# Skip term of a selective-scan and feed-forward block: transposes of a scaled x in place of products with a diagonal, and jobs placed anew

## The chip, the cores and the metric

One core of one Trainium2 chip runs the whole program. The metric is the device time of one execution in microseconds, the median of several runs. A time is also given for the profiled execution, because the rows of the trace belong to that one.

## The reference, cut to what matters

```python
# x: (16, 1024, 256); W_xproj: (96, 256); W_dt: (256, 64); 16 states per channel
xz = einsum('btd,pd->btp', x, W_xproj)            # 64 rank columns, 16 B, 16 C
dt = softplus(einsum('btr,dr->btd', xz[..., :64], W_dt) + b_dt)
h_t = exp(dt_t * -exp(A_log)) * h_(t-1) + dt_t * B_t * x_t      # per channel, 16 states
y_t = sum_s h_t[s] * C_t[s]
x1  = layernorm(x + y + Dp * x)                   # the skip term: (1 + Dp) * x
out = layernorm(x1 + down(silu(gate(x1)) * up(x1)))             # hidden width 768
```

The change is about the term `(1 + Dp) * x`, with `x` in channel-major layout on the way to the token-major sum `y`.

## The kernel before, in words

**Tiles and chunks.** The 16 sequences of 1,024 tokens are cut into 32 chunks of 512 tokens. A chunk in channel-major layout is 128 partitions by 2 channel halves by 512 tokens. Two chunks make one sequence: the even one starts from state zero and its last column is saved (`carry`, L528 to L531), the odd one starts from that column. Even chunks carry sixteen small copies on ScalarE that odd ones lack, and in odd chunks the scans read `h_carry`.

**Work of a chunk, by engine.** A step is one state `s` of 16.
- ScalarE (ACT) makes the decay `exp(dt * -A)` (`decay`, L533 to L544), into the PSUM tile `p_da` for nine states and into the SBUF tile `da_k` for the seven of `K_STATES`. For those seven it also multiplies `u` by B in token-major layout (`ub_t`, L562), which TensorE transposes into `p_da` (L976).
- GpSimd (POOL) multiplies `u` by the broadcast B for the other nine states (`ub`, L434), multiplies `h` by the broadcast C for thirteen states (L445), and makes `u = dt * x` once (`u_of`, L424): 23 instructions a chunk.
- VectorE (DVE) runs two scans a state (L761), the product with C for three states (L770), and parts of the norms and of the feed-forward part.
- TensorE (PE) transposes each finished state and adds it into `p_y` (`sum_states`, L1009), adds the skip term there (`skip`, L1016 to L1021), and does the projections and the feed-forward products of the chunk before and of the one before that.

**What sets the order.** Each engine's program is written out by one loop over chunks, states and four or five zones of a step. `AT` (L34) names for each job the step and the zone in which every engine that has a part in it issues it. `DA_LEAD` (L57) says how many steps ahead the decay of a `K_STATES` state is issued, `CARRY_ZONE` (L27) in which zone of a step ScalarE copies the carried column. Each engine issues in order and waits on semaphores, so a job placed early can hold up what stands behind it.

**Slots.** `ub` has `UB_SLOTS` = 3 buffers (L58). GpSimd writes `ub` three states ahead and must wait until VectorE's scan has read the buffer (`slot_freed`, L286). `p_da` has one bank per channel half: a decay or a transposed `ub_t` goes in when the scan before has read its half.

**The skip term before.** ScalarE once builds `skip_diag`, the identity scaled by `1 + Dp` per partition (L632 to L634), and TensorE waits for it ahead of its first step (L1080). `skip` then makes eight float32 products of a block of `x_t` with that diagonal, in two halves of four. A float32 product shows as two MATMUL records, a transpose as one.

## Time and profile before

| | us |
|---|---|
| median of 3 runs | 1795.29 |
| lowest and highest run | 1794.08, 1797.53 |
| the profiled execution | 1795.7 |
| its span, first to last instruction | 1793.9 |

The profiled execution is 0.4 us above the median, and its span 1.8 us shorter than its time. Its mean granted TensorE clock is 0.989 of full speed. GpSimd is busy for 1708.0 us of the span, TensorE for 1698.9, VectorE for 1640.3 and ScalarE for 1629.6: no engine stands out by its share alone. In rows of the timeline an instruction's time covers its latency too, so that neighbours overlap; how much an instruction takes of its engine is the distance between the starts of two that follow each other without an idle note. A bracket at a row's end gives the idle time ahead of it and the instruction that ended it.

### The profile page before, as it was taken

Reading aid. Unit: us, or ns where it says so; the run is one execution under the profiler, and the core shown is the slowest. Engines: PE = TensorE matmul, PEld = TensorE weight load, DVE = VectorE, ACT = ScalarE, POOL = GpSimd, SP = SyncE. Lnnn points to the kernel's source line nnn. Section 1 sums busy time; section 2 is a strip of 40 time slices with the busy share of each in tenths; the row PEclk is TensorE's granted clock in tenths of the full one; section 3 lists DMA queues with packets and bytes.
Section 4 is the critical chain, followed back from the end, with each engine's and each line's share of the span. In section 5 each row is a group of like instructions: output and inputs, shape, how many; then the busy total and the mean of one; then the engine's idle time right before and its main releaser. Section 6 shows DMA issues by size and latency. Waiting matters only on the chain.

```text
span 1793.9 us, 31118 instructions
## 1 busy us (share of the span) xinstructions
PE 1698.9 (95%) x11048; PEld 1323.3 (74%) x11048; DVE 1640.3 (91%) x1999; ACT 1629.6 (91%) x3157; POOL 1708.0 (95%) x740
## 2 busy tenths in 40 slices
PE   5799999999999999999999999999999999999997
PEld 3677787777777777787777777777777777777775
DVE  5789999999999999999999999999999999999993
ACT  5889999999999999999999999999999999999983
POOL 5999999999999999999999999999999999999980
PEclk7999999999999999999999999999999999999999
DMA  8333444324444324444324544324443324443200
GB/s 273 93 124 108 155 140 132 103 98 146 155 139 131 104 100 145 154 139 128 108 95 150 155 137 131 106 97 149 154 137 130 107 92 153 155 137 118 95 12 25
DMA packets 116637, 224.77 MB, mean 125 GB/s; under 512 B 11169, under 2 KB 45570, under 8 KB 116482
## 3 DMA queue, kind: packets, MB, share of 16 engines
q1 hardware_dynamic: 116482, 222.78, 38.5%
q8 instruction: 88, 1.44, 0.3%
q14 instruction: 67, 0.55, 0.1%
HBM read 203.87 MB, written 18.87 MB: 124 GB/s over the span
## 4 chain that ended last, share of the span: by engine, by line
PE 46%; ACT 21%; DVE 18%; issue 8%; POOL 6%; DVEq 0%; DMA 0%; ACTq 0%; POOLq 0%; SPq 0%
DVE h L761 11%; PE p_y L1009 10%; PE p_o L1067 9%; PE p_m L1042 9%; PE p_da L976 7%; ACT p_da L544 5%; ACT ub_t L562 5%; ACT da_k L544 3%; DVE stats L776 3%; POOL h L445 3%; POOL ub L434 3%; PE p_m L942 3%; PE p_m L1053 2%; ACT L588 2%; PE p_c L989 2%
## 5 line engine op out<-in xcount | busy, mean ns | idle before, releaser
L445 POOL TENSOR_TENSOR h<-h,c_bc 128x1024 f32<-128x1024 f32 x416 | 980.8, 2376 | 13.1 <-DVE h L761 6.6
L434 POOL TENSOR_TENSOR ub<-u,b_bc 128x1024 f32<-128x1024 f32 x287 | 680.7, 2378 | 27.2 <-DVE u L811 20.3
L1009 PE MATMUL p_y<-ident,h 128*128 128x128 f32 x4096 | 525.7, 274 | 2.6 <-DVE h L770 1.3
L1009 PEld LDWEIGHTS p_y<-ident,h 128*128 128x128 f32 x4096 | 471.3, 142 | 60.7 <-issue 26.1
L544 ACT ACTIVATE p_da<-dt,neg_a 128x512 f32<-128x512 f32 x576 | 392.0, 684 | 54.6 <-DVE h L761 50.4
L562 ACT ACTIVATE ub_t<-u_t,bc_t 128x256 f32<-128x256 f32 x896 | 397.6, 495 | 0.5 <-PE p_da L976 0.5
L761 DVE TENSOR_TENSOR_SCAN h<-p_da,h_carry,ub 128x512 f32<-128x512 f32 x288 | 353.7, 1265 | 4.6 <-ACT p_da L544 4.1
L761 DVE TENSOR_TENSOR_SCAN h<-p_da,ub 128x512 f32<-128x512 f32 x288 | 338.4, 1206 | 17.5 <-ACT p_da L544 15.9
L1067 PE MATMUL p_o<-wt_down,hid 128*128 128x256 f32 x1488 | 339.3, 381 | 0.0
L976 PE MATMUL p_da<-ident,ub_t 128*128 128x128 f32 x1792 | 277.0, 281 | 45.2 <-DVE h L761 41.3
L544 ACT ACTIVATE da_k<-dt,neg_a 128x512 f32<-128x512 f32 x448 | 316.6, 711 | 0.0
L1067 PEld LDWEIGHTS p_o<-wt_down,hid 128*128 128x128 f32 x1488 | 275.4, 190 | 36.5
L761 DVE TENSOR_TENSOR_SCAN h<-da_k,h_carry,p_da 128x512 f32<-128x512 f32 x224 | 273.3, 1262 | 4.2 <-PE p_da L976 4.2
L976 PEld LDWEIGHTS p_da<-ident,ub_t 128*128 128x128 f32 x1792 | 202.0, 142 | 101.7 <-DVE h L761 60.3
L761 DVE TENSOR_TENSOR_SCAN h<-da_k,p_da 128x512 f32<-128x512 f32 x224 | 259.7, 1203 | 9.8 <-PE p_da L976 9.7
L1053 PE MATMUL p_m<-x_t,wt_up 128*128 128x512 f16 x744 | 181.2, 379 | 2.7 <-DVE hid L795 0.6
L1042 PE MATMUL p_m<-x_t,wt_gate 128*128 128x512 f16 x744 | 171.2, 380 | 7.2 <-DVE x_t L790 7.2
L795 DVE SCALAR_TENSOR_TENSOR hid<-p_m,hid 128x512 f32<-128x512 f32 x186 | 123.1, 676 | 56.6 <-PE p_m L1053 56.6
L584 ACT ACTIVATE hid<-p_m 128x512 f32<-128x512 f32 x186 | 107.7, 596 | 27.7 <-PE p_m L1042 25.4
L1042 PEld LDWEIGHTS p_m<-x_t,wt_gate 128*128 128x128 f16 x744 | 64.1, 98 | 91.8 <-ACT hid L584 19.7
L1053 PEld LDWEIGHTS p_m<-x_t,wt_up 128*128 128x128 f16 x744 | 65.2, 98 | 81.9 <-ACT hid L584 19.7
L770 DVE TENSOR_TENSOR h<-h,p_c 128x1024 f32<-128x1024 f32 x96 | 114.7, 1195 | 0.1
(98 smaller groups left out, 1585.9 us busy)
## 6 DMA issues: line engine op xcount, KB each, us to landing
c_bc<-bc_rows_dram SPq DMA_DIRECT2D x416, 256.0 KB, 5.0
b_bc<-bc_rows_dram SPq DMA_DIRECT2D x96, 512.0 KB, 5.5
b_bc<-bc_rows_dram SPq DMA_DIRECT2D x32, 768.0 KB, 4.0
x_in<-in_L_attn_x SPq DMA_DIRECT2D x32, 512.0 KB, 6.8
out_x<-res_n SPq DMA_DIRECT2D x31, 512.0 KB, 3.4
bc_rows_dram<-bc_rows SPq DMA_DIRECT2D x32, 64.0 KB, 1.6
hid<-in_L_ffn_w_gate SPq DMA_DIRECT2D x1, 768.0 KB, 4.9
hid<-in_L_ffn_w_up SPq DMA_DIRECT2D x1, 768.0 KB, 6.7
```

What stands on the lines that cost most here:

```text
L434: nc.gpsimd.tensor_tensor(ub[:, ub_slot(c, i), :, :], u[:, par, :, :], b_bc[:, i:i + 1, :].broadcast_to([P, DH, T]), ALU.mult).then_inc(s_ ...
L445: nc.gpsimd.tensor_tensor(h[:, s % H_SLOTS, :, :], h[:, s % H_SLOTS, :, :], c_bc[:, i:i + 1, :].broadcast_to([P, DH, T]), ALU.mult).then_i ...
L544: nc.scalar.activation(da, dt[:, par, q, :], ACT.Exp, scale=neg_a[:, q, s:s + 1]).then_inc(done, 1)
L562: nc.scalar.activation(ub_t[:, k_slot(c, i), k, :], u_t[:, k, :], ACT.Identity, scale=bc_t[:, par, k, s:s + 1]).then_inc(s_ubt, 1)
L761: nc.vector.tensor_tensor_scan(h[:, s % H_SLOTS, q, :], da, dbx, initial, ALU.mult, ALU.add).then_inc(s_scan, 1)
L770: nc.vector.tensor_tensor(h[:, s % H_SLOTS, :, :], h[:, s % H_SLOTS, :, :], p_c[:, :, :].broadcast_to([P, DH, T]), ALU.mult).then_inc(s_hc ...
L795: nc.vector.scalar_tensor_tensor(hid[:, j, :], p_m[:, j % 2, :] if bank is None else bank, 1.0 / (QUANT * X1_SCALE), hid[:, j, :], ALU.mul ...
L976: ins = nc.tensor.transpose(p_da[:, q, k * P:(k + 1) * P], ub_t[:, k_slot(c, i), k, q * P:(q + 1) * P], ident[:, :])
L1009: ins = nc.tensor.matmul(p_y_tok[:, k, q * P:(q + 1) * P], h[:, s % H_SLOTS, q, k * P:(k + 1) * P], ident[:, :], start=(s == SUM_ORDER[0] ...
L1042: ins = nc.tensor.matmul(p_m[:, j % 2, :], wt_gate[:, n % DH, j * P:(j + 1) * P], x1_t[:, n // DH, n % DH, :], start=(n == 0), stop=(n == ...
L1053: ins = nc.tensor.matmul(p_m[:, j % 2, :], wt_up[:, n % DH, j * P:(j + 1) * P], x1_t[:, n // DH, n % DH, :], start=(n == 0), stop=(n == 2 ...
L1067: ins = nc.tensor.matmul(p_o[:, k % 2, :], hid[:, j, k * P:(k + 1) * P], wt_down[:, j, :], start=(j == 0), stop=(j == NH - 1))
```

## The change

- The diagonal goes. ScalarE scales each channel half of `x_t` by `1 + Dp` into a new tile `x_s` (jobs `x_scaled0` and `x_scaled1`, two instructions of 128x512 in each chunk), and `skip` adds plain transposes of `x_s` into `p_y`.
- TensorE waits for `x_s` in `skip`, ScalarE waits for the previous chunk's `skip` before it overwrites `x_s`.
- `UB_SLOTS` goes from 3 to 4, `CARRY_ZONE` from 2 to 3 (the copy of the carried column stands behind the last decay of the step), `LATE` from 12 to 14.
- The decay of state 13 is issued one step ahead of it, not two (`DA_LEAD`).
- Most jobs of `AT` get other steps or zones.

```diff
-CARRY_ZONE = 2
+CARRY_ZONE = 3
...
-    "weights": (7, 1), "x_transposed": (0, 3), "x_out": (0, 0), "project": (1, 4), "rank_out": (2, 2),
+    "weights": (7, 1), "x_transposed": (0, 4), "x_out": (0, 1), "project": (2, 4), "rank_out": (3, 1),
...
+    "hidden4": (15, 0), "hidden5": (15, 0), "skip0": (8, 4), "skip1": (7, 2), "x_scaled0": (3, 1),
+    "x_scaled1": (1, 1), "down0": (1, 0), "down1": (1, 2), "down2": (1, 2), "down3": (2, 0), "down4": (3, 1),
...
-LATE = 12
+LATE = 14
 STORE_AT = 10
-DA_LEAD = {3: 2, 6: 3, 7: 3, 10: 3, 13: 2, 14: 2}
-UB_SLOTS = 3
+DA_LEAD = {3: 2, 6: 3, 7: 3, 10: 3, 14: 2}
+UB_SLOTS = 4
...
-        skip_diag = sb("skip_diag", [P, DH, P], F32)
+        x_s = sb("x_s", [P, DH, T], F32)
...
+            def x_scaled(c, par, q):
+                act.wait_ge(s_xt, c + 1)
+                if first_wait(act, s_skip, 2 * c):
+                    act.wait_ge(s_skip, 2 * c)
+                nc.scalar.mul(x_s[:, q, :], x_t[:, par, q, :], skip1[:, q:q + 1]).then_inc(s_xs, 1)
...
-            act.wait_ge(s_const, 1)
-            for q in range(DH):
-                nc.scalar.mul(skip_diag[:, q, :], ident[:, :], skip1[:, q:q + 1]).then_inc(s_skip_diag, 1)
...
             def skip(c, par, a):
+                if first_wait(pe, s_xs, 2 * (c + 1)):
+                    pe.wait_ge(s_xs, 2 * (c + 1))
                 for k in range(2 * a, 2 * a + 2):
                     for q in range(DH):
-                        nc.tensor.matmul(p_y_tok[:, k, q * P:(q + 1) * P],
-                                         x_t[:, par, q, k * P:(k + 1) * P], skip_diag[:, q, :],
-                                         start=False, stop=False, skip_group_check=True)
+                        ins = nc.tensor.matmul(p_y_tok[:, k, q * P:(q + 1) * P],
+                                               x_s[:, q, k * P:(k + 1) * P], ident[:, :],
+                                               start=False, stop=False, is_transpose=True, skip_group_check=True)
+                ins.then_inc(s_skip, 1)
...
-            pe.wait_ge(s_skip_diag, 2)
```

How the order of the instructions moves, at three places of a chunk in the middle of the program. The line numbers in the rows of the changed kernel are its own: L552 is the decay, L570 `ub_t`, L539 the carried column, L505 `rank_out`, L514 `bc_out`, L575 `z_out`, L501 `x_scaled`.

**ScalarE, steps 1 to 3 of an even chunk.** Before, from the first decay of state 2 on:

```order
L544 ACTIVATE p_da<-dt,neg_a 128x512
L544 ACTIVATE da_k<-dt,neg_a 128x512
L562 ACTIVATE ub_t<-u_t,bc_t 128x256 x2
L531 COPY h_carry<-h 128x2
L544 ACTIVATE p_da<-dt,neg_a 128x512
L544 ACTIVATE da_k<-dt,neg_a 128x512
L506 COPY bc_rows<-p_m 32x512
L567 COPY z<-p_y 128x1024
L497 COPY rank_t<-p_m 64x512
L531 COPY h_carry<-h 128x2
```

Now:

```order
L501 ACTIVATE x_s<-x_t,skip 128x512
L552 ACTIVATE p_da<-dt,neg_a 128x512
L552 ACTIVATE da_k<-dt,neg_a 128x512
L570 ACTIVATE ub_t<-u_t,bc_t 128x256 x2
L552 ACTIVATE p_da<-dt,neg_a 128x512
L552 ACTIVATE da_k<-dt,neg_a 128x512
L539 COPY h_carry<-h 128x2
L575 COPY z<-p_y 128x1024
L539 COPY h_carry<-h 128x2
L501 ACTIVATE x_s<-x_t,skip 128x512
L505 COPY rank_t<-p_m 64x512
L514 COPY bc_rows<-p_m 32x512
```

One scaling stands ahead of the decay of state 2, the other behind the copy of `z`; the two copies out of the projection have moved behind both.

**ScalarE, steps 10 and 11 of an even chunk, behind the table load that follows the last silu.** Before:

```order
L588 ACT_TABLE_LOAD
L544 ACTIVATE p_da<-dt,neg_a 128x512
L531 COPY h_carry<-h 128x2
L544 ACTIVATE p_da<-dt,neg_a 128x512
L562 ACTIVATE ub_t<-u_t,bc_t 128x256 x2
L544 ACTIVATE p_da<-dt,neg_a 128x512
L544 ACTIVATE da_k<-dt,neg_a 128x512
L562 ACTIVATE ub_t<-u_t,bc_t 128x256 x2
L531 COPY h_carry<-h 128x2
L544 ACTIVATE p_da<-dt,neg_a 128x512
```

Now:

```order
L596 ACT_TABLE_LOAD
L552 ACTIVATE p_da<-dt,neg_a 128x512 x2
L539 COPY h_carry<-h 128x2
L570 ACTIVATE ub_t<-u_t,bc_t 128x256 x2
L552 ACTIVATE p_da<-dt,neg_a 128x512
L570 ACTIVATE ub_t<-u_t,bc_t 128x256 x2
L552 ACTIVATE p_da<-dt,neg_a 128x512
L539 COPY h_carry<-h 128x2
L570 ACTIVATE ub_t<-u_t,bc_t 128x256 x2
L552 ACTIVATE da_k<-dt,neg_a 128x512 x2
```

The `da_k` here, the decay of state 13, has left; the second decay of state 12 (the last `p_da` row) now stands ahead of the column of state 11 (the last `h_carry` row).

**TensorE, steps 0 to 3, from the transposes of the next chunk's x on.** Before:

```order
L935 MATMUL p_m<-ident,x_in 128x128 x8
L1067 MATMUL p_o<-wt_down,hid 128x256 x9
L1009 MATMUL p_y<-ident,h 128x128 x8
L942 MATMUL p_m<-x_t,wt_proj 96x512 x2
L1009 MATMUL p_y<-ident,h 128x128 x8
L976 MATMUL p_da<-ident,ub_t 128x128 x8
L1067 MATMUL p_o<-wt_down,hid 128x256 x12
```

Now:

```order
L943 MATMUL p_m<-ident,x_in 128x128 x8
L1078 MATMUL p_o<-wt_down,hid 128x256 x9
L1017 MATMUL p_y<-ident,h 128x128 x16
L1078 MATMUL p_o<-wt_down,hid 128x256 x3
L984 MATMUL p_da<-ident,ub_t 128x128 x4
L950 MATMUL p_m<-x_t,wt_proj 96x512 x2
L984 MATMUL p_da<-ident,ub_t 128x128 x4
L1078 MATMUL p_o<-wt_down,hid 128x256 x12
```

The projection has moved from ahead of the transposes for state 3 (`p_da`) to between their two halves, and one group of three down products, which stood ahead of the transposes of `x_in`, now stands ahead of the first half.

## Rows read from the trace of the kernel before

**Rows 1.** The page, part 1: busy time, share, instructions of each engine.
```profile
PE 1698.9 (95%) x11048; PEld 1323.3 (74%) x11048; DVE 1640.3 (91%) x1999; ACT 1629.6 (91%) x3157; POOL 1708.0 (95%) x740
```

**Rows 2.** Waits of POOL over the whole span: total us, times, longest us.
```profile
POOL ub L434 <- DVE h L761: 6.9, 16, 1.1
POOL h L445 <- ACT h_carry L531: 6.5, 16, 0.4
```

**Rows 3.** Timeline of POOL, around its two waits of a chunk pair.
```profile
822.53 2.38 POOL L445 TENSOR_TENSOR h<-h,c_bc 128x1024 f32<-128x1024 f32 x1 [0.41 <-ACT h_carry L531]
...
868.97 2.36 POOL L424 TENSOR_TENSOR u<-dt,x_t 128x1024 f32<-128x1024 f32 x1
...
1623.01 2.36 POOL L424 TENSOR_TENSOR u<-dt,x_t 128x1024 f32<-128x1024 f32 x1
...
1644.31 2.36 POOL L434 TENSOR_TENSOR ub<-u,b_bc 128x1024 f32<-128x1024 f32 x1 [0.35 <-DVE h L761]
```

**Rows 4.** The page, part 4: the chain that ended last, by engine.
```profile
PE 46%; ACT 21%; DVE 18%; issue 8%; POOL 6%; DVEq 0%; DMA 0%; ACTq 0%; POOLq 0%; SPq 0%
```

**Rows 5.** Timeline of PE in an even chunk: a skip half between transposes.
```profile
910.26 1.06 PE L1019 MATMUL p_y<-skip_diag,x_t 128*128 128x128 f32 x8
911.16 1.04 PE L1009 MATMUL p_y<-ident,h 128*128 128x128 f32 x8
912.03 1.06 PE L1019 MATMUL p_y<-skip_diag,x_t 128*128 128x128 f32 x8
```

**Rows 6.** Timeline of ACT, from the end of an odd chunk into the even one.
```profile
888.98 1.01 ACT L493 COPY x_t<-p_m 128x1024 f32<-128x1024 f32 x1 [0.31 <-PE p_m L935]
...
892.44 0.69 ACT L544 ACTIVATE p_da<-dt,neg_a 128x512 f32<-128x512 f32 x1 [0.33 <-DVE h L761]
893.07 0.71 ACT L544 ACTIVATE da_k<-dt,neg_a 128x512 f32<-128x512 f32 x1
...
895.19 0.71 ACT L544 ACTIVATE da_k<-dt,neg_a 128x512 f32<-128x512 f32 x1
895.93 0.58 ACT L506 COPY bc_rows<-p_m 32x512 f32<-32x512 f32 x1
...
900.58 0.89 ACT L562 ACTIVATE ub_t<-u_t,bc_t 128x256 f32<-128x256 f32 x2
901.55 0.69 ACT L544 ACTIVATE p_da<-dt,neg_a 128x512 f32<-128x512 f32 x1
```

**Rows 7.** Timeline of DVE, from state 12 of an even chunk to state 3.
```profile
930.78 1.22 DVE L761 TENSOR_TENSOR_SCAN h<-p_da,ub 128x512 f32<-128x512 f32 x1 [0.19 <-ACT p_da L544]
...
950.55 2.45 DVE L761 TENSOR_TENSOR_SCAN h<-da_k,h_carry,p_da 128x512 f32<-128x512 f32 x2 [0.17 <-PE p_da L976]
```

**Rows 8.** Timeline of PE in steps 0 to 2 of an odd chunk.
```profile
942.56 4.05 PE L1067 MATMUL p_o<-wt_down,hid 128*128 128x256 f32 x18
946.45 1.04 PE L1009 MATMUL p_y<-ident,h 128*128 128x128 f32 x8
947.32 1.88 PE L942 MATMUL p_m<-x_t,wt_proj 128*96 128x512 f32 x4
949.04 1.04 PE L1009 MATMUL p_y<-ident,h 128*128 128x128 f32 x8
```

**Rows 9.** Timeline of PE at the start of the program.
```profile
26.28 1.97 PE L935 MATMUL p_m<-ident,x_in 128*128 128x128 f32 x8 [1.27 <-ACT skip_diag L634]
```

**Rows 10.** Timeline of PE in the second chunk: first, second and last of fourteen rows, all transposes.
```profile
68.92 1.86 PE L1009 MATMUL p_y<-ident,h 128*128 128x128 f32 x8
70.62 1.04 PE L976 MATMUL p_da<-ident,ub_t 128*128 128x128 f32 x8
...
79.06 1.04 PE L935 MATMUL p_m<-ident,x_in 128*128 128x128 f32 x8
```

**Rows 11.** Stretches: busy time (count) of PE, PEld, DVE, ACT, POOL; granted clock; DMA.
```profile
68.00:72.00 4.00, 4.00 (x27) 4.00 (x26) 0.74 (x1) 3.45 (x8) 4.00 (x3) 0.68 0.48 128
...
76.00:80.00 4.00, 4.00 (x36) 3.86 (x36) 4.00 (x4) 3.06 (x7) 4.00 (x3) 1.00 0.30 66
```

More of the change, by code:

```diff
@@ L34 @@
 AT = {
[L35 to L39 removed]
[9 rows of a table removed]
+    "weights": (7, 1), "x_transposed": (0, 4), "x_out": (0, 1), "project": (2, 4), "rank_out": (3, 1),
+    "bc_out": (3, 1), "project_dt": (3, 4), "softplus_abs": (5, 1), "softplus_exp": (5, 3),
+    "softplus_log": (6, 2), "dt_of": (8, 0), "u_of": (11, 1), "u_transposed0": (11, 1), "u_out0": (13, 3),
+    "u_transposed1": (14, 3), "u_out1": (14, 3), "z_out": (2, 1), "stats1": (3, 2), "mean1": (4, 2),
+    "norm_log": (5, 1), "norm_exp": (6, 0), "shifts": (6, 1), "norm1_0": (6, 3), "norm1_1": (7, 0),
[9 rows of a table added]
+    "norm2_3": (15, 3), "bc_turned": (8, 2), "bc_cols": (10, 1),
 }
@@ L643, in step @@
                             x_out(c + 1, 1 - par)
+                        for q in range(DH):
+                            if core and due(f"x_scaled{q}"):
+                                x_scaled(c, par, q)
                         if nxt and due("rank_out"):
```

7 lines of the change are left out of this document (2 added, 5 removed), and 16 rows, old and new, of the table AT.

## The prediction

> **What bounds the kernel now.** I read the shares first. GpSimd has the most, 1708.0 us, and TensorE the next, 1698.9 [rows 1]: no engine is far enough ahead to be the bound by its share alone. The waits of GpSimd come second, since it leads. In the middle of the program it runs without a gap except for two short waits in each pair of chunks. In the even chunk the product with C of state 11 waits 0.41 us for the carried column that ScalarE copies, and at the start of the even chunk a `ub` waits 0.35 us for VectorE's scan to free one of three buffers [rows 3]. Over the whole span these are 16 waits of each kind, 6.5 and 6.9 us [rows 2], together 13.4 us.
>
> From its wait to the next `u` GpSimd issues twenty instructions, 868.97 - 822.53 = 46.44 us, or 2.322 us each. A pair of chunks has 46 of them, 106.8 us. The pair really takes (1623.01 - 868.97) / 7 = 107.72 us [rows 3]; the two waits are 0.76 of the difference. So there are two limits close together: GpSimd's own work, and a ring through the other engines that is some 0.8 us a pair longer and makes GpSimd wait. The chain of waits says the same: PE has 46% of it, ACT 21%, DVE 18% and POOL 6% [rows 4]. What the change can gain is what it takes off that ring, and at most the 13.4 us of GpSimd's waits.
>
> I followed the ring through one pair in the timelines. From the end of the odd chunk's step 11 VectorE works to the first states of the even chunk. Then ScalarE has the ring, from its wait for VectorE at 892.44 [rows 6] through the decays, the softplus and the norm to the high part of x1. After it come VectorE's low part, the gate products on TensorE, the silu, a table load and the decays of states 11 and 12. Then VectorE again, from its scan at 930.78 to that of state 3 at 950.55 [rows 7], and on to `dt_of`; then TensorE with the transposes of x1 and the gates of the odd chunk.
>
> **TensorE loses work where it isn't the bound.** Half a skip term takes 911.16 - 910.26 = 0.90 us, four products. Eight transposes take 912.03 - 911.16 = 0.87 us [rows 5], so four take 0.44. The skip is two halves a chunk: 2 x (0.90 - 0.44) = 0.92 us less a chunk, 29 us over 32 chunks. I count it at nothing. Both halves stand ahead of the transposes of x1, and these wait for VectorE's `dt_of`, which comes later than the skip; the second half now stands behind them, where a group of four transposes (`bc_turned`) of the same length has left. If TensorE were the ring in steps 7 and 8, the whole 29 us would come off, so the bounds are 0 and 29, cut by GpSimd's reserve to 13.4.
>
> **ScalarE gains two scalings a chunk.** The nearest row is a decay of the same shape, SBUF to SBUF with a scale per partition: its neighbours start 893.07 - 892.44 = 0.63 us apart [rows 6]. Two make 1.26 us a chunk, 40 us over the span. Where they go decides. The first stands just ahead of the decay that waited 0.33 us for VectorE, and the copy of `x_t` before it, which waited 0.31 us for TensorE, no longer has to, since three down products have left the place ahead of those transposes. Together 0.64 against 0.63: it costs nothing. The second stands behind the copy of `z`. Between there and the decay of state 5 I find two gaps that it can fill. The copy of B and C began 895.93 - 895.19 = 0.74 us after its neighbour where a decay takes 0.63, a gap of 0.11, and the decay at 901.55 starts 0.97 us after two `ub_t` that last 0.89 and, like the decays (0.69 against 0.63), overlap the next by 0.06, a gap of 0.14 [rows 6]. The rest, 0.63 - 0.25 = 0.38 us, is partly absorbed by smaller gaps; I take 0.2. In the odd chunk VectorE's scans are longer and ScalarE waits for them in steps 1 to 5, so there both are hidden. Bounds for the pair: 0 (all absorbed) and 4 x 0.63 = 2.5 us (none).
>
> **The decays of states 12 and 13.** The first decay of state 13 leaves the stretch behind the table load and the second decay of state 12 moves up by one instruction. VectorE waited 0.19 us for exactly that one [rows 7]; the wait goes, and the row behind it is VectorE's continuous work, so 0.19 us come off the ring. The carried column of state 11 doesn't move: one decay left ahead of it and another came. State 13's decay is now just in time, perhaps 0.1 us late for its second half; bounds -0.19 and +0.1.
>
> **The projection between the two halves for state 3.** VectorE waited 0.17 us for the first half [rows 7]. Of the work ahead of it the projection leaves, 949.04 - 947.32 = 1.72 us, and three down products come, a third of 946.45 - 942.56 = 3.89 us, so 1.30 [rows 8]: 0.42 us earlier, the wait goes. The second half comes 1.3 us later than now, but VectorE needs it only after its first scan, half of 2.45 us on [rows 7]; it just holds. Bounds: -0.17, and some +0.3 if it doesn't.
>
> **Slots and the carried column.** With four buffers GpSimd no longer waits at 1644.31 [rows 3]. That alone buys nothing: it then reaches state 11 of the even chunk earlier and waits there for the ring, up to the whole difference. That wait is what is late next. `LATE` leaves the order of SyncE's transfers in the middle as it is: 0 us.
>
> **The start.** TensorE waited 1.27 us for the diagonal ahead of the first transposes of `x_in` [rows 9]. That goes, and about 1 us of it is kept by the ring, since GpSimd's first wait there was short. I count 1 us.
>
> **Sum.** A pair: +0.2 - 0.19 - 0.17 = -0.16 us by the terms alone, 0 to -0.36 with the second scaling between fully paid and free. The copies behind the projection and the copy of x moved as well and leave ScalarE's small gaps fewer, so I take -0.25. Over 15.5 pairs that is -3.9 us, with the start -4.9: the profiled execution's 1795.7 becomes 1790.8. That execution is 0.4 above the median of 1795.29, so I give 1790.5 us.
>
> GpSimd's share is the highest and the change leaves its 1708.0 / 2.322, or some 735, long instructions as they are. The Trainium skill (Perfetto Trace Analysis, Identifying the Most-Contended Engine) tells one to improve the engine with the highest occupancy first; by that alone the sum would be zero and the time 1795.3. The chain [rows 4] speaks against taking it so far, since GpSimd also waits.
>
> **Rivals.**
> 1. **GpSimd alone bounds.** The rearrangement takes more off the ring than I find, 0.8 us a pair or more, and all waits of [rows 2] go: 1795.3 - 13.4 = 1782. For it: 29 us leave TensorE, whose share is the second highest. Against: its waits for `dt_of`. 0.20.
> 2. **No change.** The second scaling is paid in full, or a scaling stretches the ring as much as the two short waits give back: 1793 to 1797. For it: every term is under 0.4 us a pair. 0.22.
> 3. **Slower, ScalarE in the even chunk.** ScalarE has the ring from 892.44 on, and the even chunk also has sixteen column copies. If neither scaling finds a gap there, both stand whole ahead of the high part of x1: 1.26 - 0.36 = +0.9 us a pair, 14 us, 1809; from about 0.36 us a pair not absorbed the time rises. For it: ScalarE's rows follow each other there with gaps of at most 0.2. Against: the waits of 0.31 and 0.33 just ahead. 0.10.
> 4. **Clock.** Between the projection for dt and the gates TensorE now runs transposes alone, where two skip halves of products stood. Were that to lower the granted clock, transposes would cost twice: eight took 70.62 - 68.92 = 1.70 us [rows 10] at a clock of 0.68 in that stretch [rows 11], against 0.87 at full clock [rows 5]. Paid for the eight of the skip alone that is 0.83 x 32 = 27 us, 1822. Against it stand fourteen rows of transposes alone in the second chunk, from 68.92 to 79.06 [rows 10], in which the clock came up from 0.68 to 1.00 [rows 11] and stayed. 0.03.
>
> The Trainium skill (TensorE: Matmul & The Clock Gate, Part 4: PE-mode transpose) says that transposes do not count as busy in the same way and do not bring the full clock. By that rule rival 4 would be the likeliest; this trace disagrees, with its 1.00 through transposes alone.
>
> **How the numbers follow.** My forecast, 1787 to 1794, has 0.45; rivals 1 to 4 have 0.20, 0.22, 0.10 and 0.03. What can be told from no change is about 0.2%, 3.6 us: faster means below 1791.7. That is all of rival 1 and three quarters of the forecast, 0.54. Within are the rest of the forecast and nearly all of rival 2, 0.31. Slower: rivals 3 and 4 and a little of rival 2, 0.15. The range takes in rival 1 from 1783 and rival 2 to 1797 and leaves out rivals 3 and 4 and the edge of rival 1.
>
> **What would show it.** GpSimd's 16 waits for a scan are gone, those for the carried column stay and are longer, some 0.5 us each; the pair takes 107.4 to 107.5. VectorE's waits of 0.19 and 0.17 are gone. TensorE is busy some 29 us less and idles more ahead of the x1 transposes; ScalarE is busy some 40 us more. The clock stays at 1.00. It is wrong if GpSimd waits nowhere in the middle (rival 1), if the pair is still 107.7, or if ScalarE needs over 9.7 us in an even chunk from the first decay of state 2 to that of state 5 (901.55 - 892.44 = 9.11 now, 9.3 by my sum), which is rival 3.

## The result, and the profile after

The changed kernel takes 1811.42 us, the median of four runs (1811.3 to 1812.09), beside 1795.68 for the kernel before (four runs, 1794.08 to 1797.53): a ratio of 1.0084, 95% interval 1.0072 to 1.0096. It is 15.7 us slower. I had forecast 1790.5 and a range up to 1797. The profiled execution is one of 1811.3 us with a span of 1809.5, 15.6 more than before.

The page's part 1 and part 4, as in [rows 1] and [rows 4]:

```profile
PE 1663.0 (92%) x10792; PEld 1288.2 (71%) x10792; DVE 1650.2 (91%) x1999; ACT 1664.8 (92%) x3219; POOL 1708.6 (94%) x740
...
POOL 56%; issue 19%; ACT 12%; PE 7%; DVE 5%; DMA 0%; POOLq 0%; DVEq 0%; ACTq 0%; SPq 0%
```

TensorE is busy 36 us less, ScalarE 35 us more, GpSimd as long as before. The chain by engine now says GpSimd, where it said TensorE. That reads like a bound that has moved to GpSimd, and it is misleading: GpSimd does the same 1708 us of work in a span 15.6 us longer. Its waits for the carried column, 6.5 us in 16 before [rows 2], tell what it is waiting for. The same view after:

```profile
POOL h L447 <- ACT h_carry L539: 26.0, 33, 2.1
```

In each pair it waits twice now, where it waited 0.41 us once for the column and 0.35 for a slot [rows 3]. The timeline of GpSimd in an even chunk:

```profile
828.25 2.36 POOL L447 TENSOR_TENSOR h<-h,c_bc 128x1024 f32<-128x1024 f32 x1 [0.99 <-ACT h_carry L539]
...
831.17 2.38 POOL L447 TENSOR_TENSOR h<-h,c_bc 128x1024 f32<-128x1024 f32 x1 [0.56 <-ACT h_carry L539]
```

**The clock didn't change.** Busy time (count) of PE, PEld, DVE, ACT, POOL, granted clock, DMA share and GB/s, from 100 to 1700 us, of the kernel before and then of the change:

```profile
100.00:1700.00 1600.00, 1556.29 (x10220) 1215.23 (x10221) 1511.33 (x1831) 1499.10 (x2906) 1587.71 (x684) 1.00 0.40 127
```

```profile
100.00:1700.00 1600.00, 1509.34 (x9889) 1170.75 (x9890) 1508.10 (x1820) 1521.87 (x2945) 1574.55 (x678) 1.00 0.40 127
```

**Where in the program the time is.** VectorE does `dt` once a chunk, so its rows are marks that both kernels share. The second, the fourth and the last of 32 marks before, then after:

```profile
49.91 1.20 DVE L734 SCALAR_TENSOR_TENSOR dt<-p_m,dt 128x1024 f32<-128x1024 f32 x1
...
157.82 1.20 DVE L734 SCALAR_TENSOR_TENSOR dt<-p_m,dt 128x1024 f32<-128x1024 f32 x1
...
1665.86 1.19 DVE L734 SCALAR_TENSOR_TENSOR dt<-p_m,dt 128x1024 f32<-128x1024 f32 x1
```

```profile
50.52 1.20 DVE L742 SCALAR_TENSOR_TENSOR dt<-p_m,dt 128x1024 f32<-128x1024 f32 x1
...
161.79 1.20 DVE L742 SCALAR_TENSOR_TENSOR dt<-p_m,dt 128x1024 f32<-128x1024 f32 x1
...
1681.51 1.20 DVE L742 SCALAR_TENSOR_TENSOR dt<-p_m,dt 128x1024 f32<-128x1024 f32 x1
```

At the fourth mark the change is 3.97 us behind, at the last 15.65, 14 pairs later, and from there on nothing is added. So a pair costs (15.65 - 3.97) / 14 = 0.83 us more, and about 3.1 of the first 3.97 come from the start.

**The pair, in halves.** The first hidden tile of each chunk is a row of VectorE with a wait of over 1.5 us for the gate and up products. In the middle these rows repeat to 0.01 or 0.02 us from most pairs to the next (one pair is 0.12 us longer before and 0.36 after), so the instructions of two kernels can be laid beside each other from such a row on. The first half runs from the hidden tile of the even chunk to that of the odd one, the second half from there to the next even chunk's. Before, they last 53.73 and 53.97 us, with the change 54.01 and 54.50: +0.28 and +0.53.

VectorE's rows with waits after, from 771.20 (the start of a second half) on; the last two belong to the next first half:

```profile
803.17 0.69 DVE L810 SCALAR_TENSOR_TENSOR res<-p_o,x 128x512 f32<-128x512 f32 x1 [0.16 <-PE p_o L1078]
...
809.84 0.16 DVE L793 SCALAR_TENSOR_TENSOR shift<-mean_var,p_c 128x8 f32<-128x8 f32 x1 [0.67 <-ACT p_c L613]
...
817.13 1.23 DVE L798 SCALAR_TENSOR_TENSOR x_t<-p_m,x_t 128x1024 f16<-128x1024 f32 x1 [0.42 <-ACT x_t L588]
...
825.70 0.69 DVE L803 SCALAR_TENSOR_TENSOR hid<-p_m,hid 128x512 f32<-128x512 f32 x1 [1.75 <-PE p_m L1064]
...
834.64 1.22 DVE L769 TENSOR_TENSOR_SCAN h<-da_k,p_da 128x512 f32<-128x512 f32 x1 [0.30 <-ACT da_k L552]
```

The waits of [rows 7] are gone, as foreseen. In their place stands 0.30 us for the decay of state 13, now just in time, and 0.67 us for ScalarE at the shifts. The low part of x1 waits for ScalarE in either kernel. So in the second half VectorE goes by ScalarE, and ScalarE's rows decide. Before:

```profile
784.74 0.69 ACT L544 ACTIVATE p_da<-dt,neg_a 128x512 f32<-128x512 f32 x1 [0.33 <-DVE h L761]
...
789.72 0.58 ACT L497 COPY rank_t<-p_m 64x512 f32<-64x512 f32 x1
...
807.50 1.00 ACT L580 ACTIVATE x_t<-p_m 128x1024 f16<-128x1024 f32 x1
```

And after:

```profile
787.25 0.69 ACT L552 ACTIVATE p_da<-dt,neg_a 128x512 f32<-128x512 f32 x1 [1.57 <-DVE h L769]
...
792.11 0.71 ACT L501 ACTIVATE x_s<-x_t,skip 128x512 f32<-128x512 f32 x1
792.83 0.69 ACT L552 ACTIVATE p_da<-dt,neg_a 128x512 f32<-128x512 f32 x1
...
797.17 0.73 ACT L501 ACTIVATE x_s<-x_t,skip 128x512 f32<-128x512 f32 x1
797.80 0.57 ACT L505 COPY rank_t<-p_m 64x512 f32<-64x512 f32 x1
...
802.33 0.67 ACT L552 ACTIVATE p_da<-dt,neg_a 128x512 f32<-128x512 f32 x1
...
816.11 1.00 ACT L588 ACTIVATE x_t<-p_m 128x1024 f16<-128x1024 f32 x1
```

From the decay that VectorE releases (784.74, 792.83) to the high part of x1, ScalarE runs without an idle note: 22.76 us before, 23.28 after, 0.52 more. The instructions between are the same but for one scaling, in another order. The decay itself stands 21.64 and 21.63 us after the half's first row, so it is VectorE that sets it in both, though the row after has no note: the first scaling has filled the wait. That 0.52 is the second half's 0.53. Why it is 0.52, when a scaling takes 0.63 and I had priced it at 0.2, and what the first half and the start lose, is what the experiments are about.

### The profile page after: what moved, and what is told of

It is laid out like the page before. It is cut to its first block, busy times and chain, and to the rows that moved or that the text cites. A ratio compares the mean times of both kernels' runs of the same rounds, so it can differ in the third digit from the quotient of the medians.

```text
span 1809.5 us, 30715 instructions
## 1 busy us (share of the span) xinstructions
PE 1663.0 (92%) x10792; PEld 1288.2 (71%) x10792; DVE 1650.2 (91%) x1999; ACT 1664.8 (92%) x3219; POOL 1708.6 (94%) x740
## 4 chain that ended last, share of the span: by engine, by line
POOL 56%; issue 19%; ACT 12%; PE 7%; DVE 5%; DMA 0%; POOLq 0%; DVEq 0%; ACTq 0%; SPq 0%
POOL h L447 29%; POOL ub L436 24%; DVE h L769 4%; ACT ub_t L570 3%; POOL u L426 3%; ACT p_da L552 2%; ACT da_k L552 2%; PE p_m L1053 2%; PE p_o L1078 1%; PE p_da L984 1%; PE p_y L1017 1%; ACT L596 1%; PE p_m L950 1%; DVE hid L803 0%; DVE h L778 0%
## 5 line engine op out<-in xcount | busy, mean ns | idle before, releaser
L552 ACT ACTIVATE p_da<-dt,neg_a 128x512 f32<-128x512 f32 x576 | 389.1, 679 | 50.3 <-DVE h L769 48.3
L570 ACT ACTIVATE ub_t<-u_t,bc_t 128x256 f32<-128x256 f32 x896 | 401.5, 496 | 0.2 <-PE p_da L984 0.2
L552 ACT ACTIVATE da_k<-dt,neg_a 128x512 f32<-128x512 f32 x448 | 312.5, 711 | 0.8
L1064 PE MATMUL p_m<-x_t,wt_up 128*128 128x512 f16 x744 | 186.2, 379 | 2.7 <-DVE hid L803 0.6
```

Source lines behind the costliest of these rows:

```text
L552: nc.scalar.activation(da, dt[:, par, q, :], ACT.Exp, scale=neg_a[:, q, s:s + 1]).then_inc(done, 1)
L570: nc.scalar.activation(ub_t[:, k_slot(c, i), k, :], u_t[:, k, :], ACT.Identity, scale=bc_t[:, par, k, s:s + 1]).then_inc(s_ubt, 1)
L1064: ins = nc.tensor.matmul(p_m[:, j % 2, :], wt_up[:, n % DH, j * P:(j + 1) * P], x1_t[:, n // DH, n % DH, :], start=(n == 0), stop=(n == 2 ...
```

## The experiments

All times are medians; the ratio is to the kernel before, timed beside each run, with its 95% interval. The halves come from the traces. "The ring" is the loop of waits from engine to engine that sets how long a pair takes.

| run | us | ratio | first half | second half |
|---|---|---|---|---|
| before | 1795.7 to 1796.9 | 1 | 53.73 | 53.97 |
| the change | 1811.42 | 1.0084 [1.0072, 1.0096] | 54.01 | 54.50 |
| e1 skip alone | 1804.93 | 1.0045 [1.003, 1.006] | 53.73 | 54.56 |
| e2 placement alone | 1812.07 | 1.0084 [1.0069, 1.0099] | 54.28 | 54.28 |
| e3 one scaling | 1808.44 | 1.0063 [1.0046, 1.0079] | 54.00 | 54.27 |
| e4 root early | 1818.2 | 1.0117 [1.0102, 1.0132] | 54.28 | 54.70 |
| e5 skip alone, scaled in step 15 | 1797.85 | 1.0008 [0.9999, 1.0018] | 53.89 | 53.98 |
| e6 transposes, no scaling | 1795.71 | 0.9994 [0.9985, 1.0004] | 53.73 | 53.98 |
| e7 decay 13 two ahead | 1823.8 | 1.015 [1.0135, 1.0165] | 54.89 | 54.51 |
| e8 residual early | 1811.0 | 1.0078 [1.0061, 1.0095] | 54.05 | 54.51 |
| e9 the change, scaled in step 15 | 1818.48 | 1.0128 [1.0111, 1.0145] | 54.36 | 54.63 |
| e10 e9, projection back | 1837.29 | 1.0231 [1.0216, 1.0246] | 55.49 | 55.14 |
| e11 four slots alone | 1796.75 | 1.0006 [0.9996, 1.0015] | 53.74 | 53.98 |
| e12 decays 13, 14 one ahead alone | 1797.85 | 1.0006 [0.9996, 1.0015] | 53.95 | 53.98 |
| e13 both scalings at (15, 1) | 1807.12 | 1.0056 [1.0041, 1.0071] | 54.00 | 54.27 |
| e14 e13, rank behind decays | 1821.1 | 1.0136 [1.0121, 1.0151] | 54.54 | 54.66 |
| e15 e14, decay 13, column back | 1834.42 | 1.0211 [1.0196, 1.0227] | 54.72 | 55.22 |
| e16 skip alone, both at (15, 1) | 1803.76 | 1.0036 [1.0023, 1.0048] | 54.08 | 53.99 |
| e17 projection late alone | 1809.47 | 1.0071 [1.0056, 1.0086] | 53.93 | 54.25 |
| e18 e13, steps 0 to 2 back | 1802.88 | 1.0038 [1.0023, 1.0052] | 54.15 | 54.00 |

The texts on record use letters. S says that the second scaling lengthens ScalarE's run ahead of the high part of x1. R says that the reciprocal root, now behind the softplus exp, makes VectorE wait at the shifts. D says that state 13's decay, now just in time, is the loss. L, the rival in e5, says that ScalarE's extra work costs the same wherever it stands.

### The two parts of the change apart (e1, e2, e6)

e1 is the kernel before with the skip change, and with the scalings at the change's steps, nothing else placed anew:

```diff
-    ... "skip0": (8, 0), "skip1": (7, 2), "down0": (0, 2), ...
+    ... "skip0": (8, 0), "skip1": (7, 2), "x_scaled0": (3, 1), "x_scaled1": (1, 1), "down0": (0, 2), ...
```

> The kernel before with the skip change alone: x_scaled1 at (1, 1), x_scaled0 at (3, 1), transposes in skip, no diagonal; table, slots and lags as before. Theory S (the two scalings lengthen ScalarE's stretch in the even chunk, the high part of x1 comes about 0.5 us a pair later): 15.5 x 0.5, about +8 us, 1803, up to 1811 if they lie there whole. Theory R (the reciprocal deviation was moved behind the softplus exp, and VectorE waits 0.67 us a pair for it in shifts): nothing of it is here, 1795. Theory D (the decay of state 13 one step later holds up VectorE by 0.30 us a pair): nothing of it here, 1795.

Measured 1804.93, as S had it: 8 us lost by the skip change alone. ScalarE's rows from the scaling ahead of the released decay to the high part of x1:

```profile
787.08 0.71 ACT L500 ACTIVATE x_s<-x_t,skip 128x512 f32<-128x512 f32 x1
787.69 0.68 ACT L551 ACTIVATE p_da<-dt,neg_a 128x512 f32<-128x512 f32 x1
...
793.24 0.72 ACT L500 ACTIVATE x_s<-x_t,skip 128x512 f32<-128x512 f32 x1
...
810.85 1.01 ACT L587 ACTIVATE x_t<-p_m 128x1024 f16<-128x1024 f32 x1
```

The decay comes 21.82 us after the half's first row instead of 21.64: the first scaling is hidden but for 0.18. The run from it is 810.85 - 787.69 = 23.16 instead of 22.76: the second scaling costs 0.40. Together 0.58 a pair. In the odd chunk, the first half, both are hidden (53.73).

e2 has the change's placement with the diagonal and the products back:

```diff
-                                               x_s[:, q, k * P:(k + 1) * P], ident[:, :],
-                                               start=False, stop=False, is_transpose=True, skip_group_check=True)
+                                               x_t[:, par, q, k * P:(k + 1) * P], skip_diag[:, q, :],
+                                               start=False, stop=False, skip_group_check=True)
```

> The changed kernel with the skip term of before: the diagonal and eight products, no scalings; table, slots and lags of the change. Theory S: the scalings are gone, about 8 us less than the change, 1803. Theory R alone: 1811, as the change. Theory D alone: 1811.

Measured 1812.07, so S is not the whole cause: the placement costs as much alone as the whole change, and the two parts' costs (8 and 16 us) don't add. Its first half is 0.27 longer than the change's. There the skip's products stand behind the transposes of x1 and ahead of gates that are waited for: from these transposes to the first gate product it takes 3.98 us in e2 and 3.52 in the change. This is the one place where TensorE's relief is worth something, and the change made that place itself.

e6 keeps the old placement and makes transposes of `x_t` itself, so that ScalarE has no scaling to do and the factor `1 + Dp` is missing from the output:

```diff
-                                         x_t[:, par, q, k * P:(k + 1) * P], skip_diag[:, q, :],
-                                         start=False, stop=False, skip_group_check=True)
+                                         x_t[:, par, q, k * P:(k + 1) * P], ident[:, :],
+                                         start=False, stop=False, is_transpose=True, skip_group_check=True)
```

> The kernel before with the skip's eight products replaced by transposes of x unscaled: the factor 1 + Dp is left out, nothing is added to ScalarE. It measures what TensorE's 0.92 us a chunk are worth in the old placement. Prediction of record: nothing, 1796 to 1797. Rival: TensorE is in the ring in steps 7 and 8, up to GpSimd's reserve, 1783.

Measured 1795.71. The relief of TensorE is worth nothing there. The timeline of TensorE shows where it goes, in the kernel before and then in e6:

```profile
859.88 1.06 PE L1032 MATMUL p_m<-ident,x 128*128 128x128 f32 x8 [0.23 <-DVE dt L734]
```

```profile
861.59 1.06 PE L1032 MATMUL p_m<-ident,x 128*128 128x128 f32 x8 [1.15 <-DVE dt L734]
```

The idle time ahead of the transposes of x1 grows by 0.92 us, which is all that two skip halves gave up.

### Where a scaling costs (e3, e5, e9, e13, e16)

e3 is the change without `x_scaled0`:

```diff
-                        for q in range(DH):
+                        for q in range(1, DH):
                             if core and due(f"x_scaled{q}"):
```

> The changed kernel with x_scaled0, the scaling behind the copy of z, left out; channel half 0 is transposed from x unscaled, so its factor 1 + Dp is missing from the output. Theory S: this is the scaling that finds too few gaps, so its 0.5 us a pair go, 1803 to 1804. Theories R and D: 1811.

Measured 1808.44, where S had 1803 to 1804: 0.23 a pair less than the change. The second scaling costs only that much here, because `rank_t` behind it waits 0.27 us for TensorE's projection once it is gone. That wait was the first sign of the second cause.

e5 is e1 with the scalings in step 15 of the chunk before, for the next chunk's x:

```diff
+                        for q in range(DH):
+                            if nxt and due(f"x_scaled{q}"):
+                                x_scaled(c + 1, 1 - par, q)
```

> The kernel before with the skip change alone, but the x of the next chunk is scaled in step 15, at (15, 1) and (15, 3), where ScalarE waits 0.88 and 0.42 us for VectorE at the end of an odd chunk and 0.34 and 0.36 at the end of an even one. Theory S (a scaling costs where ScalarE has the ring, not by itself): the 0.6 us a pair of e1 go, the time is that of the kernel before, 1796, or a microsecond less from the start. Rival L (ScalarE's load as such costs, 1.26 us a chunk wherever it stands): 1805, as e1.

Measured 1797.85, within 0.2% of the kernel before: S right, L wrong. The second half is 53.98, untouched. The first lost 0.16, since a scaling at (15, 1) makes VectorE wait for a decay:

```profile
727.36 1.28 DVE L770 TENSOR_TENSOR_SCAN h<-p_da,h_carry,ub 128x512 f32<-128x512 f32 x1 [0.29 <-ACT p_da L551]
```

e9 does the same to the change: `"x_scaled0": (15, 1), "x_scaled1": (15, 3)`.

> The change, with both scalings of a chunk's x moved from its own steps 1 and 3 to step 15 of the chunk before. Theory S+P (the scaling costs what stands between ScalarE's copies and the high part of x1; the later projection and its copies cost the rest, and the two overlap): the even chunk loses 0.2 to 0.25 us of its 54.50, the pair is at 108.3, the time 1807 to 1809, still 10 us and more over the kernel before. If the scaling were the whole cause, as it nearly was in the kernel before with the skip alone: 1797 to 1798.

A miss: 1818.48, slower than the change by 7 us. The wait at the shifts went from 0.67 to 0.43 us, so ScalarE's run did lose its scaling. But in the new placement the scaling at (15, 3) falls between two decays that VectorE needs (0.25 us of wait in each chunk), and that costs more. Two things were moved into one step at once, and only one place in it was free.

e13 puts both ahead of the first decay of that zone:

```diff
-    "hidden4": (15, 0), "hidden5": (15, 0), "skip0": (8, 4), "skip1": (7, 2), "x_scaled0": (3, 1),
-    "x_scaled1": (1, 1), ...
+    "hidden4": (15, 0), "hidden5": (15, 0), "skip0": (8, 4), "skip1": (7, 2), "x_scaled0": (15, 1),
+    "x_scaled1": (15, 1), ...
```

> The change, with both scalings at (15, 1) of the chunk before, ahead of the decay in that zone, where ScalarE idles for 1.57 us (second half) and 1.07 us (first half) in the trace of the change. Theory T (what counts is the unbroken run of ScalarE from the decay at 21.6 us to the high part of x1): the run loses 0.62 us of scaling and gets the wait at rank_t back (0.27), so the second half goes from 54.50 to about 54.2, the first stays at 54.0 to 54.1, the pair is 108.2 to 108.3, the time 1806 to 1809. If scalings cost VectorE 0.25 us a chunk wherever they stand in step 15, as in the run at (15, 1) and (15, 3): 1818.

Measured 1807.12, halves 54.00 and 54.27, all as expected. ScalarE's rows in the second half:

```profile
787.85 0.69 ACT L552 ACTIVATE p_da<-dt,neg_a 128x512 f32<-128x512 f32 x1 [0.35 <-DVE h L771]
...
793.44 0.69 ACT L552 ACTIVATE p_da<-dt,neg_a 128x512 f32<-128x512 f32 x1 [0.63 <-DVE h L771]
...
797.69 0.20 ACT L539 COPY h_carry<-h 128x2 f32<-128x2 f32 x1
798.16 0.58 ACT L505 COPY rank_t<-p_m 64x512 f32<-64x512 f32 x1 [0.27 <-PE p_m L952]
...
816.47 1.00 ACT L588 ACTIVATE x_t<-p_m 128x1024 f16<-128x1024 f32 x1
```

The idle 1.57 us has become 0.35: two scalings went into a gap that was there. The run from 793.44 to 816.47 is 23.03, 0.27 over the kernel before, and it holds a wait of 0.27. With the scaling in the run it was 23.28. So the change's 0.52 is 0.27 for the late projection and 0.25 for the scaling. The rest of the scaling's 0.63, 0.38 us, went into the wait: counted from start to start, `rank_t` begins 798.16 - 797.69 = 0.47 us after a column copy that takes 0.09 in the change (797.08 to 797.17), so 0.38 are lost there, where the note says 0.27. That the run grows by just the 0.27 of the note is partly chance, since other small gaps of the old order have closed. Both scalings free give back 4.3 of the 15.7 us, not more.

e16 does the same to the old placement, where the gap ahead of that decay is shorter: `"x_scaled0": (15, 1), "x_scaled1": (15, 1)` in e5.

> The kernel before with the skip change alone and both scalings at (15, 1) of the chunk before. Theory T: the wait of 0.29 us that the scaling at (15, 1) brought VectorE in the odd chunk's ring shrinks or stays, since there ScalarE idles only 0.35 us ahead of its first decay: pair 107.7 to 107.95, time 1796 to 1799, no gain over the kernel before in either case.

Slower than expected, 1803.76. The wait grew from 0.29 to 0.47 us in the first half:

```profile
729.68 2.46 DVE L770 TENSOR_TENSOR_SCAN h<-p_da,h_carry,ub 128x512 f32<-128x512 f32 x2 [0.47 <-ACT p_da L551]
```

The same edit gained 11.4 us in the new placement (e9 to e13) and lost 5.9 in the old one (e5 to e16). Of the 5.9 the halves show 0.20 a pair, some 3 us; where the rest comes from is open.

### VectorE's new waits, one at a time (e4, e7, e8)

e4 puts the reciprocal root ahead of the softplus exp, for the 0.67 us at the shifts: `-"norm_exp": (6, 0)`, `+"norm_exp": (5, 2)`.

> The changed kernel with norm_exp at (5, 2) in place of (6, 0), so that the reciprocal deviation is made ahead of the softplus exp, as before. Theory R: VectorE's 0.67 us wait in shifts goes, 15.5 x 0.67 = 10 us less, 1801. Theory S: the wait in shifts goes too, but VectorE then only waits longer for the high part of x1 (0.42 us now, 1.1 then), time unchanged, 1811.

R fell: 1818.2, 7 us worse. The wait at the shifts is gone and the next one, at the low part of x1, is 1.22 us instead of 0.42. The 0.67 us on VectorE were slack: the low part of x1 waits for the end of ScalarE's run anyway, and the run got longer, its end 45.11 us after the half's first row instead of 44.91. In the first half the low part, which waits for nothing in the change, now waits 0.41 us.

e7 gives state 13's decay its old lead, for the 0.30 us: `+DA_LEAD = {3: 2, 6: 3, 7: 3, 10: 3, 13: 2, 14: 2}`.

> The changed kernel with the decay of state 13 two steps ahead again. Theory D: VectorE's wait of 0.30 us a pair for it goes and nothing comes, 15.5 x 0.3 = 5 us less, 1807. Rival: the first half of it then stands ahead of the second decay of state 12 and the carried column in ScalarE's stretch again, and the time stays 1811 or rises.

Worse, 1823.8, and the first half is 54.89. VectorE's wait of 0.30 us did go: its next hidden tiles behind state 13 begin 13.23 us after the half's first row instead of 13.43. But with `CARRY_ZONE` 3 the decay stands ahead of the carried column of state 11, which comes 6.43 us after the half's first row instead of 5.21. GpSimd, TensorE and VectorE, in this order:

```profile
728.56 2.37 POOL L447 TENSOR_TENSOR h<-h,c_bc 128x1024 f32<-128x1024 f32 x1 [1.77 <-ACT h_carry L539]
```

```profile
737.96 1.09 PE L1017 MATMUL p_y<-ident,h 128*128 128x128 f32 x8 [0.89 <-POOL h L447]
```

```profile
746.89 0.69 DVE L810 SCALAR_TENSOR_TENSOR res<-p_o,x 128x512 f32<-128x512 f32 x1 [1.29 <-PE p_o L1078]
```

Here GpSimd's wait has become long enough for TensorE to wait for GpSimd, and the down products behind it on TensorE come late. So 1.77 us of wait for the carried column are no longer free, where up to 0.95 are (e11 below). And e7 says nothing against D: it gained D's 0.2 us and lost more in another place. What D is worth, e12 shows.

e8 puts the second residual back: `-"residual1": (5, 0)`, `+"residual1": (4, 2)`.

> The changed kernel with the second residual at (4, 2) in place of (5, 0), so that the means of the first norm stand between it and the statistics that read it. In the change residual, statistics and scan start 0.72 and 1.44 us apart where they took 0.58 and 1.41: 0.2 us in each chunk. In the odd chunk VectorE has the ring there: 0.2 a pair, 3 us less, 1808. In the even chunk ScalarE has it: nothing. Rival (VectorE just waits for the shift's input instead): 1811.

No gain, 1811.0, the change's time within the noise: the residual then waits 0.25 us for the down products, which come later as well.

### Slots and leads in the kernel before (e11, e12)

e11 is `-UB_SLOTS = 3`, `+UB_SLOTS = 4` in the kernel before.

> The kernel before with four buffers for GpSimd's products in place of three, nothing else. Theory: GpSimd's slot waits (6.9 us in 16) turn into waits for the carried column (6.5 in 16 become 13), and the time stays at 1796, within 1 us. If a slot wait had held the ring: 0.4 us a chunk, so 1790.

Measured 1796.75, as expected. The slot waits are gone, the one for the column grew to 0.75 to 0.95 us in the middle of the program.

e12 adds `-DA_LEAD = {3: 2, 6: 3, 7: 3, 10: 3, 13: 2, 14: 2}`, `+DA_LEAD = {3: 2, 6: 3, 7: 3, 10: 3}`.

> The kernel before with four buffers and the decays of states 13 and 14 one state ahead, not two. Theory of the ring (VectorE's two waits of 0.19 and 0.17 us in the odd chunk end, with nothing else moved that feeds it): 0.19 to 0.36 us a pair less, 1790 to 1793. If the decays then come late for states 13 or 14 of GpSimd's or VectorE's products: 1796 or more.

No gain, 1797.85. The wait of 0.19 us ends and one of 0.41 takes its place:

```profile
720.60 1.22 DVE L761 TENSOR_TENSOR_SCAN h<-da_k,p_da 128x512 f32<-128x512 f32 x1 [0.41 <-ACT da_k L544]
```

This time it is state 14 that waits. The first half is 53.95, 0.21 over e11's 53.74, and 0.41 - 0.19 is 0.22: VectorE's rows stay that much later from state 14 to the end of the half. So in the first half a wait of VectorE for a decay counts in full. By the same count the change's 0.30 us at state 13, less the 0.19 that it replaced, is +0.11 us a pair, and VectorE's hidden tiles behind it do begin 0.11 us later (13.43 for 13.32). e12's total hides its loss, because at the fourth mark of `dt` it is 2.3 us ahead of the kernel before.

### The projection (e10, e14, e15, e17, e18)

e10 puts the projection of e9 back ahead of the transposes for state 3:

```diff
-    ... "project": (2, 4), "rank_out": (3, 1), "bc_out": (3, 1), ... "z_out": (2, 1), ...
+    ... "project": (1, 4), "rank_out": (2, 2), "bc_out": (2, 0), ... "z_out": (2, 2), ...
```

> The run before it, with the projection and its three copies put back at the places they have in the kernel before: project at (1, 4), rank_out at (2, 2), bc_out at (2, 0), z_out at (2, 2). Theory P (the new place of the projection is what the other moves cost): the first absolute value of the softplus comes back to 34.9 us after the first hidden tile of the chunk before, from 35.4, the pair to 107.9 to 108.0, the time 1799 to 1802. If another of the moves is the cause (the softplus exp ahead of the reciprocal root, the residual or the state 13 decay in step 3): within 2 us of the run before it.

A miss by far, 1837.29. The change has also moved down products from ahead of that place to behind it, and now they stand behind the projection; the residual waits for them, 1.34 us in the first half and 1.19 in the second:

```profile
750.65 0.69 DVE L812 SCALAR_TENSOR_TENSOR res<-p_o,x 128x512 f32<-128x512 f32 x1 [1.34 <-PE p_o L1080]
```

e14 lets e13's `rank_t` stand behind a pair of decays: `-"rank_out": (3, 1)`, `+"rank_out": (3, 3)`, and `bc_out` alike.

> The run before it, with rank_out and bc_out at (3, 3), behind the first decays of step 3, in place of (3, 1). Theory T: the wait of 0.27 to 0.6 us at rank_t goes, since the decays stand ahead of it, and the second half comes to 53.95 to 54.0: 107.9 to 108.1, the time 1801 to 1805. Rival: rank_t then comes 1.2 us later, project_dt with it, and the first absolute value of the softplus waits for TensorE instead: no gain, or a loss of up to 0.3 us a pair, 1808 to 1812.

Neither theory nor rival as they stood: 1821.1. The wait only changed hands, because the decays need VectorE's scan there:

```profile
801.64 0.69 ACT L552 ACTIVATE p_da<-dt,neg_a 128x512 f32<-128x512 f32 x1 [0.67 <-DVE h L771]
...
802.88 0.56 ACT L505 COPY rank_t<-p_m 64x512 f32<-64x512 f32 x1
```

The two copies, 1.1 us of work, had filled the time in which that scan ran. Before, the copy of B and C did so ahead of `z`, since the projection was done.

e15 adds `CARRY_ZONE = 2` and state 13's lead of two to e14.

> The run before it, with state 13's decay two ahead and the carried column in zone 2, both as in the kernel before. In the first half VectorE's wait of 0.30 us at state 13 goes and one or two of 0.19 come back: 0.1 to 0.3 us a pair less than the run before it. The carried column stands ahead of the decays again, so the late columns that made the run with state 13 two ahead slow (1823.8) don't come. 1798 to 1804. If the 0.28 us of the first half come from the later down products and the residual instead: equal to the run before it, within 1.5 us.

1834.42, a miss. In the second half the four instructions that scale and shift the first norm now stand behind a carried column that waits 0.38 us for VectorE, and the high part of x1 is 0.6 us later than in e14. I had judged the two settings apart from the placement around them.

e17 makes the projection late in the kernel before, and nothing else:

```diff
-    ... "project": (1, 4), "rank_out": (2, 2), "bc_out": (2, 0), ... "z_out": (2, 2), ...
+    ... "project": (2, 4), "rank_out": (3, 1), "bc_out": (3, 1), ... "z_out": (2, 1), ...
```

> The kernel before with project at (2, 4), rank_out and bc_out at (3, 1) and z_out at (2, 1), the places of the change, and nothing else of it. Theory T: rank_t waits for the projection, ScalarE's run up to the high part of x1 gets 0.2 to 0.5 us longer in the second half of the ring, the pair is at 107.9 to 108.2, the time 1800 to 1804. If the late projection costs nothing by itself: 1796 to 1797.

This is the run that settles it. ScalarE's rows in the second half:

```profile
792.14 0.69 ACT L544 ACTIVATE p_da<-dt,neg_a 128x512 f32<-128x512 f32 x1 [0.33 <-DVE h L761]
...
796.86 0.58 ACT L497 COPY rank_t<-p_m 64x512 f32<-64x512 f32 x1 [0.27 <-PE p_m L942]
...
815.17 1.00 ACT L580 ACTIVATE x_t<-p_m 128x1024 f16<-128x1024 f32 x1
```

The run is 23.03, exactly e13's, with the same wait of 0.27. e17 moves the projection together with the three copies behind it, and no run moves it alone, but it is TensorE's projection that `rank_t` waits for. The first half has 0.20 more and a wait of 0.59 at `rank_t`. There, too, down products come later behind the projection, and VectorE's second residual, which had no wait before, begins 0.16 us later:

```profile
748.53 0.69 DVE L802 SCALAR_TENSOR_TENSOR res<-p_o,x 128x512 f32<-128x512 f32 x1 [0.25 <-PE p_o L1067]
```

The two halves together are 0.48 of the change's 0.81 a pair in the middle of the program. The time, 1809.47, is above what I expected, because the start pays as well: at the fourth mark of `dt` e17 is 4.8 us behind the kernel before. In the change's own trace the start reads so, TensorE first, then ScalarE:

```profile
32.35 1.12 PE L984 MATMUL p_da<-ident,ub_t 128*128 128x128 f32 x4 [5.86 <-ACT ub_t L570]
33.26 3.61 PE L950 MATMUL p_m<-x_t,wt_proj 128*96 128x512 f32 x4
```

```profile
36.90 0.58 ACT L505 COPY rank_t<-p_m 64x512 f32<-64x512 f32 x1 [1.92 <-PE p_m L950]
```

The projection is in line behind transposes that wait 5.86 us for `ub_t`, while its own operand has long been there, and ScalarE waits 1.92 us for it. A little later VectorE's wait for the transposes of a state is 3.80 us before and 5.47 after:

```profile
71.26 2.33 DVE L761 TENSOR_TENSOR_SCAN h<-da_k,p_da 128x512 f32<-128x512 f32 x2 [3.80 <-PE p_da L976]
```

```profile
72.81 2.33 DVE L769 TENSOR_TENSOR_SCAN h<-da_k,p_da 128x512 f32<-128x512 f32 x2 [5.47 <-PE p_da L984]
```

e18 is e13 with steps 0 to 2 as in the kernel before: `x_transposed`, `x_out`, `project`, `rank_out`, `bc_out`, `z_out`, and `down0` to `down3`.

> The change with both scalings at (15, 1) (1807.1) and, as in the kernel before, x_transposed, x_out, project, rank_out, bc_out, z_out and the first four down products. Theory T: the residual doesn't wait 1.2 us as it did with the projection alone put back, the wait at rank_t is gone, the second half goes from 54.27 to 53.95 to 54.05, the pair to 107.9 to 108.1, the time 1800 to 1804; the 0.28 us of the first half stay. If what is left comes from steps 3 to 15: 1806 to 1808.

Measured 1802.88, as expected. The second half is back at 54.00, and the 1.2 us of the residual are gone: put back together with the down products ahead of it, and the transposes of x, the projection does no harm there, and without them it did (e10). The first half is longer, 54.15, with VectorE's 0.29 us for state 13 and 0.37 for the transposes of state 3.

## Why the prediction was wrong

**What held.** TensorE's relief counted at nothing (e6). The clock stayed at 1.00, so rival 4 fell. The slot waits are gone, worth nothing alone (e11), and come back as waits for the column. VectorE's 0.19 and 0.17 us are gone as foreseen.

**The scalings.** Of the second one I wrote "The rest, 0.63 - 0.25 = 0.38 us, is partly absorbed by smaller gaps; I take 0.2." In the old placement it costs 0.40 (e1), near the 0.38 but not by my sum: of the two gaps only the one ahead of the decay of state 5 lies behind the scaling there and closes, 0.17 us from start to start; the rest is hundredths. In the change it costs 0.25, near my 0.2, and that is luck: what swallowed the rest was the wait at `rank_t`, which the change itself opened and I hadn't seen. "it costs nothing" for the first holds in the change, where the released decay stands where it stood. In e1 it costs 0.18, since the copy of `x_t` still waits there (0.32 us) and only the wait ahead of the decay can take the scaling. Together the two cost 0.25 a pair in the change, 4.3 us by e13 and 3 by e3.

**The projection: the step that failed.** I weighed its move by what it does for the transposes for state 3 ("0.42 us earlier, the wait goes") and never by who waits for the projection itself. That is ScalarE's `rank_t`, inside the very run that I had named as the ring. I even booked the moved copies as a gain ("leave ScalarE's small gaps fewer, so I take -0.25"), where they are a loss of 0.27 in the second half and about 0.2 in the first (e17). For the whole move I had -0.26 us a pair, and e17 measures +0.48 a pair and a start that is 4.8 us late.

**State 13.** A second step failed, a smaller one. I took off the whole 0.19 us of VectorE's wait and left its new wait, "perhaps 0.1 us late", out of the sum. It is 0.30, so the term is +0.11 and not -0.19, at the very edge of my bounds of -0.19 and +0.1 (e12 shows that such a wait counts in full).

**The start.** "I count 1 us" of gain; it is a loss of about 3. The diagonal's 1.27 us did go, and the copy of x_t began 1.75 us earlier (26.53 for 28.28). But the projection has left the place right behind it, and `rank_t` begins 1.52 us later (36.90 for 35.38). With the skip change alone the start does gain: at the fourth mark e5 is 0.98 us ahead of the kernel before, 0.26 of it already at the first.

**Sum.** Predicted -0.25 a pair and -1; measured about +0.81 and +3. A pair by the terms as measured one by one: the projection with its copies +0.48 (e17) for my -0.17 - 0.09 = -0.26, state 13 +0.11 for my -0.19, the second scaling +0.25 (e13) for my +0.2, together +0.84. Without the scaling this gives 0.59, and e13 has 0.57. The late projection alone takes the time to 1809.5 (e17).

**The rivals.** Rival 3 came closest: the right engine, the right chunk, a price of 0.9 a pair and 1809. Its mark, the stretch of 9.11 us in [rows 6], is 802.33 - 792.83 = 9.50 after, just between my 9.3 and its 9.7. But its mechanism, both scalings paid in full, isn't what happened: they cost 0.25 of the 0.81. That its time comes close is chance. Still, at 0.10 its chance was too low for a run in which the rows follow each other with gaps of at most 0.2 [rows 6]. Rival 1 fell with GpSimd's longer waits, rival 2 with the interval, which leaves out no change.

**What stays open.** The shares of the first half's 0.28 are only added up: the late projection alone makes 0.20 and state 13 0.11, but with steps 0 to 2 put back the transposes of state 3 are late (0.37 for 0.17 us) and the half is longer still (e18). So undoing the projection gives back 4.2 us (e13 to e18), much less than it costs alone. No run beats the kernel before. The nearest with the skip change is e5, at 1.0008 [0.9999, 1.0018]; since e6 gains nothing even with the scaling free, there is nothing for it to win in that placement.

## What to carry to other kernels

When a ring has been found in which each engine is just in time for the next, list for each moved job who waits for its result and whether that waiter is in the ring; a job's own wait that vanishes is the smaller half of the account. An instruction added to an unbroken run of an in-order engine costs the distance between starts that it takes, less the gaps that the starts of the rows behind it show (0.63 became 0.40 in e1); the place to put it is ahead of a row that waits longer than it takes. Put a moved job back only with the jobs that traded places with it, and don't take the engine with the longest wait, or with the largest share of the chain, for the one that sets the time: here waits of 0.67 and 0.95 us were worth nothing (e4, e11), and one of 0.27 marked the run that cost the most. When undoing a single setting makes things worse, look whether its own term came back before calling it innocent (e7).
